# A four-part transformer kernel: order tables of the first attention and of the last feed-forward part, and a split maximum

## The chip, the cores and the metric

The kernel runs on one core of a Trainium2 chip. The metric is the device time of one execution in microseconds (us), as the median of several runs. A core has five engines that run their own instruction streams and meet at semaphores: TensorE (PE: matmuls and transposes; PEld is its weight load), VectorE (DVE), ScalarE (ACT), GpSimd (POOL) and SyncE (SP), which here only issues DMAs.

## The reference

Four sublayers, each added to the residual x of 4 batches x 512 tokens x 512 channels; all in float32:

```python
x = x + tanh(g_xattn[0]) * L0_xattn(layernorm(x), ctx, wq, wk, wv, wo, ...)   # 16 heads of 128, 4 key heads, RoPE, causal, 64 context keys
x = x + tanh(g_ffn[0])   * L0_ffn(layernorm(x), ...)                          # 16 experts, top 4, and a shared expert
x = x + tanh(g_xattn[1]) * L1_xattn(layernorm(x), ctx, mask, ...)             # 16 heads of 32 over 64 context keys, int8-like q and out
x = x + tanh(g_ffn[1])   * L1_ffn(layernorm(x), w1, g1, w2, g2, w3, g3)

def L1_ffn(x):                       # D = 512, H = 2048
    h = silu(linear_bit(x, w1, g1)) * linear_bit(x, w2, g2)
    return linear_bit(h, w3, g3)
def linear_bit(x, w, g):
    xq = act_quant(rmsnorm(x, g))    # scale 127 / max|row|, clipped from below; round
    wq = round(tanh(w / mean|w|)) * arctanh(mean|w|)      # values -1, 0, 1 times a constant
    return xq @ wq.T
```

## The kernel before, in words

The first attention (`attention0_stage`) runs in 64 slots, one for a group of 4 query heads with its key head and a tile of 128 tokens; the 16 tiles of the first key head come first. Every engine walks a table of steps that is written by hand: one string for each kind of slot, where the kind is the slot's number modulo 4 (`ACT_ORDER`, `DVE_ORDER`, `POOL_ORDER`, `PE_ORDER`; the first slot and what lies before and behind the 64 have strings of their own). The kind also says how many keys a tile sees: 192, 320, 448 or 576 for the kinds 0 to 3. All matmuls of float32 data are made of three products of high and low halves. The letters that matter here, for the softmax of slot s unless said otherwise:

- `S` (PE) scores of head i into PSUM; `M` (DVE, L689) their negated maximum; `e` (ACT, L577) exp with the row sum; `N` (DVE, L714) its reciprocal, and for head 3 also the product (L717); `p` (POOL, L803) the product with the reciprocal for heads 0 and 1; `n` (ACT, L582) the same for head 2.
- `P` (PE) transposes of the probabilities of slot s-1, piece i; `g` (ACT, L592 or L589) their copy out of PSUM; `V` (PE, L954, L951) the product with the values; `o` (ACT, L596) and `B` (DVE, L743) high and low half of the result; `W` (PE) the output projection.
- `k` and `q` (PE) the projections of slot s+2; `v` on ACT (L610 to L612) squares the key half and copies the values, `v` on DVE (L748, L750) is the rotation of k, after which piece 0 of `q` may use the PSUM bank that follows. `K` and `T` (PE, L958, L963) transpose k and q of slot s+1, `k` and `t` on ACT (L600, L604) and DVE (L727, L732) copy them; the next slot's scores wait for the last of these. `f` (ACT) and `E` (DVE), `x`, `q` and `r` belong to the norms and the rotation of q.
- `w` (ACT, L561) copies the next weight block to its high half, four pieces of 128 x 512, in a slot of kind 1 (output weights, slots 1, 17, 33, 49) or kind 2 (query weights, slots 14, 30, 46); POOL's `w` (L782) makes the low half of each piece.
- `j`: work for the last sublayer rides along. In 15 slots from 2 to 22 ACT sums pieces of its weights. In 24 slots from 25 to 60 DVE turns two pieces of 128 x 512 into -1, 0 and 1 (`j0`, `j1`, each L707 and L711). In kind order 0 to 3 these are 7, 5, 5 and 7 slots.

TensorE transposes go through two PSUM banks in turn (`TR`), so that a transpose waits for the copy of the one two before it; the projections, V and W go through two banks in turn as well (`A`).

The last sublayer (`attention1_ffn1_stage`, the functions called `feed`) runs on 16 tiles of 128 tokens, again with one string per engine: `PE_FEED`, `ACT_FEED`, `DVE_FEED`, `POOL_FEED`, and joins (`DVE_JOIN` and others) for the slots in which it starts up beside the second attention. `P` (L2528) are the up and gate products in 4 pieces, `s` (ACT) the silu, `g` (DVE, L2384) the product h, `h` (POOL, L2163) h times g3, `H` (DVE, L2388 and L2392) the largest absolute value of the row of 2048, `t` (POOL, L2173, L2174) two powers of the mean square, `M` (DVE, L2396 to L2398) the scale, `r` (ACT, L2274) the rounding in two halves, `U` (PE, L2541) the transposes of that, `R` (DVE, L2405) their copies to bfloat16, `Y` (PE, L2550) the down product of 16 matmuls, and `X` (DVE, L2410) its addition to x. `T`, `x`, `c`, `b`, `m`, `q`, `y`, `v`, `a`, `z` are the norm of the following tile and the mean square.

Of the kernel before, what the change touches and what calls it, by code (L numbers as in the profile page):

```python
# [24 lines left out]
F32 = mybir.dt.float32  # L25
# [23 lines left out]
E = 16  # L49
# [75 lines left out]
def attention0_stage(nc, x, ident, tri, gates, xT, xh, xl, next_weights, next_loaded, xn_dram, x_in, ctx_in, wq_in, wk_in, wv_in, wo_in, wkc_in, wvc_in, qw_in, kw_in, g_xattn, g_ffn,  # L125
# [17 lines left out]

    ACT_ORDER = {"last": "g0 g1 g2 g3 g4 o L", -3: "z0 z1 r0 r1 r2 r3 x u w c0",
# [7 lines left out]


    DVE_SLOT = "M0 M1 N0 L D X A j0 l v M2 N1 N2 M3 N3 k t B j1 E"
    DVE_ORDER = {"last": "A0 A1 X0 D X1 r0 A2 X2 r1 A3 X3 r2 r3 B", -3: "A0 A1 X0 A2 X1 A3 X2 X3 b u c0 w0 c1 w1", -2: "v A E", -1: "z v X k t E A l", "first": "M0 M1 N0 X A v M2 N1 N2 M3 N3 k t E",
                 0: DVE_SLOT, 1: DVE_SLOT, 2: DVE_SLOT, 3: DVE_SLOT}

# [112 lines left out]
    with ExitStack() as ctx:  # L270
        s_ = Scope(nc, ctx, "a0")
        raw = s_.sb("raw", [P, KD, 512])
        whi = s_.sb("whi", [P, 2, KD, 512], F32R)
# [51 lines left out]
        A = s_.ps("A", [P, 2, 512])  # L325
# [49 lines left out]
        with nc.Block() as block:  # L375
# [136 lines left out]
            def _(act):  # L512
# [3 lines left out]
                def do(name, i, s, m):  # L516
# [4 lines left out]
                    if name == "r" and s < SLOTS and row(s, 5, i) is not None:  # L521
                        t = row(s, 5, i)
# [3 lines left out]
                    if name == "u" and (s == BEGIN or s % PERIOD == PERIOD - 3):  # L526
                        t = 0 if s == BEGIN else s + 3
# [26 lines left out]
                    if name == "w" and (s == BEGIN or s % PERIOD in (1, PERIOD - 2)):  # L554
                        part = 1 if s % PERIOD == 1 else 0
                        t = 0 if s == BEGIN else s + (2, -1)[part]
                        if live(t, 0):
                            until(act, raw_loaded, loads(part), t, m)
                            until(act, (q_full, wo_full)[part], (tile, opened)[part], t - 1, m)
                            for k in range(KD):  # L560
                                act.activation(whi[:, part, k], raw[:, k], ACT.Copy).then_inc(whi_ready, 1)  # L561
                    if name == "j" and (s, i) in SUMS:
# [1392 lines left out]
def attention1_ffn1_homes(nc, kept, right, sb):  # L1955
# [25 lines left out]
    for name, shape, dt in (  # L1981
            ("f_xq", [P, 2, 2, D], F32), ("f_cx", [P, 2, D], F32), ("over_biases", [P, 1207], F32), ("junk", [P, F1 // 512, 512], BF16),
            ("over_wo", [P, KD, D], BF16), ("h", [P, 2, F1], F32), ("hqT", [P, 2, F1 // P, P], BF16), ("over_values", [P, 1608], F32),
            ("hg", [P, 2, F1 + 1], F32), ("over_p", [P, 2], F32), ("hq", [P, 2, F1], F32)):
        h[name] = sb(kept, f"f_{name}", shape, dt)
# [9 lines left out]
def attention1_ffn1_stage(nc, x, x_loaded, ident, gates, wT, sq, bq, gsw, gbo, mask, kbd, vbd, g12, g3, w12T, w3T, at, out, prefetch, homes):  # L1995
# [21 lines left out]

    PE_FEED = "P0 P1 U0 P2 U1 P3 T0 Y0"

# [3 lines left out]

    DVE_FEED = "M0 X0 b0 g0 m0 g1 R0 g2 R1 g3 H0 x0 H1"

# [18 lines left out]
    POOL_JOIN = {13: "B0.15 s0.13 fy0.0 A0.11 fy1.0 fp0.0",  # L2044
# [40 lines left out]
    with ExitStack() as ctx:  # L2085
# [28 lines left out]
        def part(c):  # L2114
            return slice(c * 512, (c + 1) * 512)
# [4 lines left out]
        with nc.Block() as block:  # L2120
# [158 lines left out]
            def _(ve):  # L2279
# [74 lines left out]
                def feed(name, n, s):  # L2354
# [60 lines left out]
            def _(pe):  # L2415
# [96 lines left out]
                def feed(name, n, s):  # L2512
# [187 lines left out]
```

## Time and profile before

| | |
|---|---|
| median of 3 runs | 1870.31 us (1869.50 to 1870.43) |
| time of the profiled execution | 1871.33 us |
| its span, first to last instruction | 1869.5 us |
| granted TensorE clock, mean | 0.984 |
| busy PE, DVE, ACT, POOL | 93%, 63%, 56%, 52% |
| first attention (slots) | 47 to about 1000 us |
| last sublayer alone | about 1657 to 1866 us |

The shares are means over the whole span. A matmul's end is modelled, so PE's busy time is no measure of how full it is: in the slots one reads from where to where a slot lasts and which wait stands in it. A row of the timeline gives start, duration, engine, line, operation, what it writes and reads, and in brackets how long the engine stood idle before it and who ended that.

### The profile page before, as it was taken

The numbers are of one execution on the slowest core, as the hardware profiler recorded it, in microseconds if no ns is written. First come the engines' busy times: TensorE is split into PE (matmuls) and PEld (weight loads), VectorE is DVE, ScalarE is ACT, GpSimd is POOL, SyncE is SP. The second block draws the span as 40 slices with busy tenths as digits, with TensorE's granted clock in tenths as the row PEclk, the third lists the DMA queues.
The fourth block names the chain that finished last, engine by engine and source line by source line (L and its number), as shares of the span: only waits on it lengthen the run. The fifth ranks groups of instructions, "written<-read, shape, count | busy, mean of one in ns | idle before, by whom it ended". The sixth has DMA issues, their size and how long they took to land. (4 is left out here: it accounts for less than half of the span.)

```text
span 1869.5 us, 28380 instructions
## 1 busy us (share of the span) xinstructions
PE 1741.5 (93%) x10015; PEld 1355.0 (72%) x10052; DVE 1181.8 (63%) x2415; ACT 1038.8 (56%) x2334; POOL 975.1 (52%) x864
## 2 busy tenths in 40 slices
PE   6999999999999999999998999989999778879997
PEld 4777887777877778777775888879999556634443
DVE  5666555557556776567766657634334678868885
ACT  3566666655655555545554422146665367767875
POOL 5644565445654456545541100048888356657774
PEclk9999999999999999999999999999999889999999
DMA  7111111111111111012122100167889660000000
GB/s 250 48 54 51 51 36 57 55 24 51 36 41 45 51 48 50 19 32 56 53 85 92 63 23 23 45 231 209 227 247 273 160 142 1 1 7 18 24 23 23
DMA packets 113611, 141.36 MB, mean 76 GB/s; under 512 B 38000, under 2 KB 68720, under 8 KB 113280
## 3 DMA queue, kind: packets, MB, share of 16 engines
q1 hardware_dynamic: 106304, 122.76, 21.0%
q0 software_dynamic: 7168, 16.78, 4.3%
q8 instruction: 82, 1.34, 0.3%
q14 instruction: 57, 0.47, 0.1%
HBM read 104.91 MB, written 29.36 MB: 72 GB/s over the span
## 5 line engine op out<-in xcount | busy, mean ns | idle before, releaser
L787 POOL TENSOR_TENSOR a_xcl<-xT,a_xch 128x512 fp32r<-128x512 f32 x64 | 87.3, 1365 | 323.4 <-ACT a_xch L571 323.4
L689 DVE TENSOR_REDUCE a_nmax<-a_S 128x1 f32<-128x192 f32 (+3 forms) x256 | 135.5, 549 | 83.0 <-PE a_S L897 82.8
L954 PE MATMUL a_A<-a_pT,a_vf 128*128 128x512 f32 x320 | 168.0, 607 | 6.5 <-ACT a_pT L592 6.5
L577 ACT ACTIVATE a_pr_odd<-a_S,a_nmax 128x320 f32<-128x320 f32 (+1 forms) x128 | 80.6, 631 | 149.9 <-DVE a_nmax L689 149.8
L120 PE MATMUL a_A<-a_wlo,a_xch 128*128 128x512 f32 x256 | 143.9, 562 | 14.0 <-DVE a_qb L750 11.4
L577 ACT ACTIVATE a_pr_even<-a_S,a_nmax 128x192 f32<-128x192 f32 (+1 forms) x128 | 67.0, 526 | 123.7 <-DVE a_nmax L689 123.4
L120 PE MATMUL a_S<-xl,xh 128*128 128x288 f32 (+3 forms) x320 | 121.8, 381 | 9.7 <-DVE xl L732 5.0
L1612 POOL TENSOR_TENSOR e_wlo<-expert_raw,e_whi 128x1408 fp32r<-128x1408 f32 x31 | 100.3, 3235 | 50.2 <-ACT e_whi L1784 48.0
L2528 PE MATMUL f_HH<-w12T,f_f_xqT 128*128 128x512 bf16 x496 | 117.5, 383 | 6.9 <-DVE f_h L2384 3.8
L714 DVE RECIPROCAL a_rec<-a_rs 128x1 f32<-128x1 f32 x256 | 41.2, 161 | 120.1 <-ACT a_pr_odd L577 67.1
L120 PE MATMUL e_GUP<-e_xgl,e_whi 128*128 128x256 f32 (+1 forms) x384 | 110.4, 287 | 4.3 <-DVE e_xgl L1840 2.7
L2163 POOL TENSOR_TENSOR f_hg<-f_h,g 128x512 f32<-128x512 f32 x64 | 81.4, 1272 | 52.1 <-DVE f_h L2384 52.1
L121 PE MATMUL e_GUP<-e_xgh,e_wlo 128*128 128x256 f32 (+1 forms) x384 | 108.6, 283 | 0.0
L122 PE MATMUL e_GUP<-e_xgh,e_whi 128*128 128x256 f32 (+1 forms) x384 | 108.3, 282 | 0.0
L120 PE MATMUL a_A<-a_wlo,a_oth 128*128 128x512 f32 x256 | 104.2, 407 | 2.8 <-DVE a_otl L743 2.8
L592 ACT ACTIVATE a_pT<-a_TR 128x512 f32<-128x512 f32 x160 | 94.8, 593 | 11.6 <-PE a_TR L938 10.8
L122 PE MATMUL a_A<-a_whi,a_xch 128*128 128x512 f32 x256 | 100.8, 394 | 0.0
L121 PE MATMUL a_A<-a_whi,a_xcl 128*128 128x512 f32 x256 | 100.7, 393 | 0.0
L122 PE MATMUL a_A<-a_whi,a_oth 128*128 128x512 f32 x256 | 100.6, 393 | 0.0
L121 PE MATMUL a_A<-a_whi,a_otl 128*128 128x512 f32 x256 | 100.4, 392 | 0.0
L796 POOL TENSOR_TENSOR a_qa<-a_qa,a_qb 128x640 f32<-128x640 f32 x64 | 100.3, 1567 | 0.0
L121 PE MATMUL a_S<-xh,xl 128*128 128x288 f32 (+3 forms) x320 | 98.8, 309 | 0.0
(417 smaller groups left out, 5593.9 us busy)
## 6 DMA issues: line engine op xcount, KB each, us to landing
a_pw<-in_L_ffn_w_dram SPq DMA_DIRECT2D x96, 256.0 KB, 2.8
expert_raw<-in_L_ffn_w_gate_dram SPq DMA_DIRECT2D x16, 704.0 KB, 8.1
expert_raw<-in_L_ffn_w_up_dram SPq DMA_DIRECT2D x16, 704.0 KB, 9.9
expert_raw<-in_L_ffn_w_down_dram SPq DMA_DIRECT2D x16, 512.0 KB, 10.3
tern<-a_tern SPq DMA_DIRECT2D x48, 128.0 KB, 1.8
x_res<-in_x_dram SPq DMA_DIRECT2D x4, 1024.0 KB, 9.2
a_raw<-in_L_xattn_wq_dram SPq DMA_DIRECT2D x4, 1024.0 KB, 6.1
a_raw<-in_L_xattn_wo_dram SPq DMA_DIRECT2D x4, 1024.0 KB, 5.5
```

The source lines that it names most:

```text
L120: pe.matmul(out, lhs_hi, rhs_lo, start=first, stop=False)
L121: pe.matmul(out, lhs_lo, rhs_hi, start=False, stop=False)
L122: return pe.matmul(out, lhs_hi, rhs_hi, start=False, stop=last)
L577: act.activation(pr[s % 2][:, i, 0:keys(s)], pair(s, i), ACT.Exp, bias=nmax[:, s % 2, i:i + 1], accum_out=rs[:, s % 2, i:i + 1]).then_inc( ...
L592: act.activation(pT[:, i % 2], bank, ACT.Copy).then_inc(pT_ready, 1)
L689: ve.tensor_reduce(nmax[:, s % 2, i:i + 1], pair(s, i), AX.X, ALU.max, negate=True).then_inc(s_max, 1)
L787: pool.tensor_tensor(xcl[:, t % 2], xT[:, :, tok(t)], xch[:, t % 2].bitcast(F32), ALU.subtract).then_inc(xlo_ready, 1)
L796: pool.tensor_tensor(qa[:, t % 2], qa[:, t % 2], qb[:, t % 2], ALU.add).then_inc(q_add, 1)
L954: pe.matmul(bank, vf[:, par(t), i], pT[:, i % 2], start=i == 0, stop=False)
L1612: pool.tensor_tensor(wlo[e % 2][q, cs], raw[q, e % 2, cs], whi[e % 2][q, cs].bitcast(F32), ALU.subtract).then_inc(gu_lo, 1)
L2163: pool.tensor_tensor(hg[:, u, part(n)], h[:, u, part(n)], g3[:, part(n)], ALU.mult).then_inc(hg_ready, 1)
L2528: last = pe.matmul(HH[pair_of(s, n)][j][:], f_xqT[:, u, j * KD + k], w12T[j][:, k, part(n)], start=k == 0, stop=k == KD - 1)
```

## The change

Three things are changed. In the first attention the tables of ACT and DVE for the four kinds of slot get another order. On ACT the copies `g` of transposes come before the exponential `e2`, and the four weight copies `w` become steps of their own, `w0` to `w3`, spread over the slot. On DVE the two operations of `j0` move behind the rotation of k (`v`) and behind `N1`, and so ahead of `M2`; in kind 1, `M3` also comes ahead of `N2`. In the last sublayer the down product is issued as 4 and 12 matmuls with the transposes `T` of the next norm between them; DVE copies the second half of the rounded row (`R1`) before `g2`, and takes the maximum of the row's first half before `g3`; and the maximum of the second half, one reduction of 1025 columns, becomes one of 512 and one of 514.

```diff
-                 1: "x e0 e1 j0 g0 j1 v u e2 r g1 n w j2 e3 k t o f",
+                 1: "x e0 e1 j0 g0 w0 j1 v u w1 r g1 w2 e2 e3 n w3 j2 k t o f",
...
-    DVE_SLOT = "M0 M1 N0 L D X A j0 l v M2 N1 N2 M3 N3 k t B j1 E"
+    DVE_SLOT = "M0 M1 N0 L D X A l v N1 j0 M2 N2 M3 N3 k t B j1 E"
...
@@ -555,10 +555,10 @@
                         if live(t, 0):
-                            until(act, raw_loaded, loads(part), t, m)
-                            until(act, (q_full, wo_full)[part], (tile, opened)[part], t - 1, m)
-                            for k in range(KD):
-                                act.activation(whi[:, part, k], raw[:, k], ACT.Copy).then_inc(whi_ready, 1)
+                            if i == 0:
+                                until(act, raw_loaded, loads(part), t, m)
+                                until(act, (q_full, wo_full)[part], (tile, opened)[part], t - 1, m)
+                            act.activation(whi[:, part, i], raw[:, i], ACT.Copy).then_inc(whi_ready, 1)
...
-    PE_FEED = "P0 P1 U0 P2 U1 P3 T0 Y0"
+    PE_FEED = "P0 P1 U0 P2 U1 P3 Y0 T0 Y1"
...
-    DVE_FEED = "M0 X0 b0 g0 m0 g1 R0 g2 R1 g3 H0 x0 H1"
+    DVE_FEED = "M0 X0 b0 g0 m0 g1 R0 R1 g2 H0 g3 x0 H1 H2"
...
+    Y_HEAD = 4
...
                     if name == "H" and n == 1:
+                        ve.wait_ge(hg_ready, NC * s + 3)
+                        c.link(ve.tensor_reduce(hg[:, u, F1 + 1:F1 + 2], hg[:, u, part(2)], AX.X, ALU.max, apply_absolute_value=True))
+                    if name == "H" and n == 2:
                         ve.wait_ge(hg_ready, NC * s + NC)
                         c.order()
-                        c.link(ve.tensor_reduce(amh[:, u:u + 1], hg[:, u, 1024:F1 + 1], AX.X, ALU.max, apply_absolute_value=True))
+                        c.link(ve.tensor_reduce(amh[:, u:u + 1], hg[:, u, 3 * 512:F1 + 2], AX.X, ALU.max, apply_absolute_value=True))
...
                     if name == "Y":
-                        pe.wait_ge(hq_copied, 2 * (s + 1))
-                        if s > 0:
+                        pe.wait_ge(hq_copied, 2 * s + n + 1)
+                        if n == 0 and s > 0:
                             pe.wait_ge(f_x_done, s)
-                        else:
+                        elif n == 0:
                             pe.wait_ge(y_ready, NT)
-                        for k in range(F1 // P):
+                        for k in (range(Y_HEAD), range(Y_HEAD, F1 // P))[n]:
                             last = pe.matmul(Y[:], hqT[:, u, k], w3T[:, k], start=k == 0, stop=k == F1 // P - 1)
-                        last.then_inc(f_y_full, 1)
+                        if n == 1:
+                            last.then_inc(f_y_full, 1)
```

The other kinds of `ACT_ORDER` change in the same way: in kind 3, for one, `v e2 r g1 n g2` becomes `v r g1 e2 n g2`, and in kind 2 `g2` now stands before `e3`.

On DVE, slot 59 (kind 3) has these rows before, from the maxima of heads 0 and 1 to the reciprocal of head 3:

```order
L689 TENSOR_REDUCE a_nmax<-a_S 128x1 x2
L714 RECIPROCAL a_rec<-a_rs 128x1
L739 SCALAR_TENSOR_TENSOR x_res<-a_A,gates,x_res 128x512
L707 TENSOR_SCALAR a_xn<-a_pw,a_nthr 128x512
L711 SCALAR_TENSOR_TENSOR a_tern<-a_pw,a_thr,a_xn 128x512
L722 TENSOR_TENSOR xl<-a_kT,xh 128x64
L748 TENSOR_TENSOR a_qa<-a_A,a_cos_k 128x128
L750 TENSOR_TENSOR a_qb<-a_A,a_sin_k 128x128
L689 TENSOR_REDUCE a_nmax<-a_S 128x1
L714 RECIPROCAL a_rec<-a_rs 128x1 x2
L689 TENSOR_REDUCE a_nmax<-a_S 128x1
L714 RECIPROCAL a_rec<-a_rs 128x1
```

The same place on DVE in the changed kernel:

```order
L689 TENSOR_REDUCE a_nmax<-a_S 128x1 x2
L714 RECIPROCAL a_rec<-a_rs 128x1
L739 SCALAR_TENSOR_TENSOR x_res<-a_A,gates,x_res 128x512
L722 TENSOR_TENSOR xl<-a_kT,xh 128x64
L748 TENSOR_TENSOR a_qa<-a_A,a_cos_k 128x128
L750 TENSOR_TENSOR a_qb<-a_A,a_sin_k 128x128
L714 RECIPROCAL a_rec<-a_rs 128x1
L707 TENSOR_SCALAR a_xn<-a_pw,a_nthr 128x512
L711 SCALAR_TENSOR_TENSOR a_tern<-a_pw,a_thr,a_xn 128x512
L689 TENSOR_REDUCE a_nmax<-a_S 128x1
L714 RECIPROCAL a_rec<-a_rs 128x1
L689 TENSOR_REDUCE a_nmax<-a_S 128x1
```

The two operations of j0 (L707, L711) have moved from ahead of the rotation (L748, L750) to behind it and behind one reciprocal, and still stand ahead of head 2's maximum.

On ACT, slot 49 (kind 1, with the copies of output weights, L561) had them in one block ahead of head 3's exponential:

```order
L592 ACTIVATE a_pT<-a_TR 128x512
L610 ACTIVATE a_sq<-a_A 128x128
L611 ACTIVATE a_vf<-a_A 64x128
L612 ACTIVATE a_vf<-a_A 64x128
L577 ACTIVATE a_pr_odd,a_rs<-a_S,a_nmax 128x320
L589 ACTIVATE a_qT<-a_TR 64x256
L582 ACTIVATE a_pr_odd<-a_pr_odd,a_rec 128x320
L561 ACTIVATE a_whi<-a_raw 128x512 x4
L577 ACTIVATE a_pr_odd,a_rs<-a_S,a_nmax 128x320
L600 ACTIVATE xh<-a_TR 128x128
```

The same place on ACT in the changed kernel:

```order
L592 ACTIVATE a_pT<-a_TR 128x512
L561 ACTIVATE a_whi<-a_raw 128x512
L610 ACTIVATE a_sq<-a_A 128x128
L611 ACTIVATE a_vf<-a_A 64x128
L612 ACTIVATE a_vf<-a_A 64x128
L561 ACTIVATE a_whi<-a_raw 128x512
L589 ACTIVATE a_qT<-a_TR 64x256
L561 ACTIVATE a_whi<-a_raw 128x512
L577 ACTIVATE a_pr_odd,a_rs<-a_S,a_nmax 128x320 x2
L582 ACTIVATE a_pr_odd<-a_pr_odd,a_rec 128x320
L561 ACTIVATE a_whi<-a_raw 128x512
L600 ACTIVATE xh<-a_TR 128x128
```

Three of the four copies stand now ahead of the exponentials of heads 2 and 3 and one behind them, and the copy of a transpose (L589) comes before both exponentials.

On DVE, one tile of the last sublayer, from the second product h (L2384 here) to the scale, before:

```order
L2384 SCALAR_TENSOR_TENSOR f_h<-f_HH,f_al,f_sg 128x512
L2405 TENSOR_SCALAR f_hqT<-f_TB 128x1024
L2384 SCALAR_TENSOR_TENSOR f_h<-f_HH,f_al,f_sg 128x512
L2405 TENSOR_SCALAR f_hqT<-f_TB 128x1024
L2384 SCALAR_TENSOR_TENSOR f_h<-f_HH,f_al,f_sg 128x512
L2388 TENSOR_REDUCE f_hg<-f_hg 128x1
L2375 TENSOR_SCALAR f_f_xqT<-f_TB 128x1024
L2392 TENSOR_REDUCE f_ST<-f_hg 128x1
L2396 TENSOR_SCALAR f_ST<-f_ST,f_rooth 128x1
```

The same in the changed kernel, where the lines have other numbers (L2384 is L2385, L2388 is L2389, L2392 became L2392 and L2396):

```order
L2385 SCALAR_TENSOR_TENSOR f_h<-f_HH,f_al,f_sg 128x512
L2409 TENSOR_SCALAR f_hqT<-f_TB 128x1024 x2
L2385 SCALAR_TENSOR_TENSOR f_h<-f_HH,f_al,f_sg 128x512
L2389 TENSOR_REDUCE f_hg<-f_hg 128x1
L2385 SCALAR_TENSOR_TENSOR f_h<-f_HH,f_al,f_sg 128x512
L2376 TENSOR_SCALAR f_f_xqT<-f_TB 128x1024
L2392 TENSOR_REDUCE f_hg<-f_hg 128x1
L2396 TENSOR_REDUCE f_ST<-f_hg 128x1
L2400 TENSOR_SCALAR f_ST<-f_ST,f_rooth 128x1
```

Behind the last product h stand now a copy (L2376), a reduction of 512 and one of 514 columns, where a reduction of 1024, the copy and one of 1025 stood.

## Rows read from the trace of the kernel before

**Rows 1.** Windows: four slots without and with pieces, slots 47, 59, 49

```profile
core 0: us, PE busy (x) PEld busy (x) DVE busy (x) ACT busy (x) POOL busy (x), PEclk, DMA share, GB/s
702.42:760.05 57.63, 57.45 (x326) 46.66 (x326) 32.35 (x75) 34.48 (x89) 35.65 (x33) 1.00 0.13 41
882.56:944.09 61.53, 58.59 (x327) 46.62 (x326) 44.98 (x91) 31.14 (x84) 30.39 (x28) 1.00 0.19 53
744.10:760.05 15.95, 15.77 (x92) 12.62 (x91) 8.72 (x19) 8.55 (x22) 7.66 (x7) 1.00 0.00 1
926.83:944.09 17.26, 16.02 (x93) 12.53 (x91) 12.11 (x23) 8.45 (x23) 7.85 (x7) 1.00 0.16 47
776.50:790.10 13.60, 12.27 (x72) 10.20 (x71) 8.79 (x22) 9.43 (x25) 11.53 (x11) 1.00 0.13 35
```

**Rows 2.** Waits of PE in slots 56 to 59: total, times, longest

```profile
PE a_A L120 <- DVE a_qb L750: 1.9, 4, 0.6
PE a_A L954 <- ACT a_pT L592: 0.6, 1, 0.6
```

**Rows 3.** Timeline of DVE in slot 59

```profile
931.72 1.56 DVE L707 TENSOR_SCALAR a_xn<-a_pw,a_nthr 128x512 bf16<-128x512 f32 x1
933.32 1.52 DVE L711 SCALAR_TENSOR_TENSOR a_tern<-a_pw,a_thr,a_xn 128x512 bf16<-128x512 f32 x1
...
935.29 0.74 DVE L689 TENSOR_REDUCE a_nmax<-a_S 128x1 f32<-128x576 f32 x1
```

**Rows 4.** Timeline of POOL in slot 59

```profile
931.75 1.26 POOL L799 TENSOR_TENSOR a_qa<-a_qa,a_srq 128x640 f32<-128x640 f32 x1
932.96 1.33 POOL L803 TENSOR_TENSOR a_pr_odd<-a_pr_odd,a_rec 128x576 f32<-128x576 f32 x1
936.18 1.15 POOL L803 TENSOR_TENSOR a_pr_odd<-a_pr_odd,a_rec 128x576 f32<-128x576 f32 x1 [1.89 <-DVE a_rec L714]
```

**Rows 5.** Timeline of ACT in slot 59

```profile
936.07 0.74 ACT L577 ACTIVATE a_pr_odd<-a_S,a_nmax 128x576 f32<-128x576 f32 x1 [2.55 <-DVE a_nmax L689]
...
937.28 0.77 ACT L582 ACTIVATE a_pr_odd<-a_pr_odd,a_rec 128x576 f32<-128x576 f32 x1
937.95 0.59 ACT L592 ACTIVATE a_pT<-a_TR 128x512 f32<-128x512 f32 x1
```

**Rows 6.** Timeline of PE in slot 59: V2

```profile
939.80 1.02 PE L954 MATMUL a_A<-a_pT,a_vf 128*128 128x512 f32 x2
```

**Rows 7.** All instances of DVE's L707 and of L711

```profile
L707 DVE TENSOR_SCALAR a_xn<-a_pw,a_nthr x48: 476/478/1561, 420.4 to 960.9; 128x512 bf16<-128x512 f32 x48
L711 DVE SCALAR_TENSOR_TENSOR a_tern<-a_pw,a_thr,a_xn x48: 750/1136/1648, 421.6 to 961.4; 128x512 bf16<-128x512 f32 x48
```

**Rows 8.** Timelines of ACT and PE in slot 49

```profile
785.12 2.18 ACT L561 ACTIVATE a_whi<-a_raw 128x512 fp32r<-128x512 f32 x4
...
789.39 0.47 PE L120 MATMUL a_S<-xl,xh 128*128 128x448 f32 x1 [1.33 <-DVE xl L732]
```

**Rows 9.** Groups of PE, whole span: transposes of k

```profile
L958 PE MATMUL a_TR<-ident_f,a_qa 128*128 128x128 f32 x64 | 17.7, 276 | 0.9 <-ACT xT L524 0.9
```

**Rows 10.** All instances of DVE's L2396, one a tile

```profile
L2396 DVE TENSOR_SCALAR f_ST<-f_ST,f_rooth x16: 226/226/227, 1663.0 to 1856.1; 128x1 f32<-128x1 f32 x16
```

**Rows 11.** Timeline of one tile of the last sublayer

```profile
1774.71 0.62 PE L2535 MATMUL f_TB<-f_ident_h,f_f_xq 128*128 128x128 f16 x8 [0.46 <-ACT f_f_xq L2251]
...
1776.93 1.27 POOL L2163 TENSOR_TENSOR f_hg<-f_h,g 128x512 f32<-128x512 f32 x1 [0.44 <-DVE f_h L2384]
...
1778.49 1.22 DVE L2392 TENSOR_REDUCE f_ST<-f_hg 128x1 f32<-128x1025 f32 x1
1778.68 0.55 POOL L2174 TENSOR_TENSOR f_unrooth<-f_ssum,f_mhalf 128x1 f32<-128x1 f32 x1
...
1780.29 1.24 ACT L2274 ACTIVATE f_hq<-f_hg,f_big,f_rech 128x1024 f32<-128x1024 f32 x1 [2.25 <-DVE f_rech L2397]
```

**Rows 12.** Timeline of PE at the end

```profile
1858.94 0.62 PE L2541 MATMUL f_TB<-f_ident_h,f_hq 128*128 128x128 f16 x8 [0.51 <-ACT f_hq L2274]
1860.75 4.82 PE L2550 MATMUL f_Y<-w3T,f_hqT 128*128 128x512 bf16 x15 [1.18 <-DVE f_hqT L2405]
```

More of the change, by code:

```diff
@@ L140, in attention0_stage @@
                 3: "S0 S1 W0 W1 W2 W3 P0 k0 k1 S2 R P1 V0 q0 P2 V1 S3 P3 K V2 q1 T V3 q2 q3"}
-    ACT_ORDER = {"last": "g0 g1 g2 g3 g4 o L", -3: "z0 z1 r0 r1 r2 r3 x u w c0",
+    ACT_ORDER = {"last": "g0 g1 g2 g3 g4 o L", -3: "z0 z1 r0 r1 r2 r3 x u w0 w1 w2 w3 c0",
                  -2: "c1 x v h0 f h1",
@@ L147, in attention0_stage @@
                  "first": "x e0 e1 v d1 r e2 n e3 k t f",
[4 rows of a table removed]
-    DVE_SLOT = "M0 M1 N0 L D X A j0 l v M2 N1 N2 M3 N3 k t B j1 E"
[4 rows of a table added]
+    DVE_SLOT = "M0 M1 N0 L D X A l v N1 j0 M2 N2 M3 N3 k t B j1 E"
     DVE_ORDER = {"last": "A0 A1 X0 D X1 r0 A2 X2 r1 A3 X3 r2 r3 B", -3: "A0 A1 X0 A2 X1 A3 X2 X3 b u c0 w0 c1 w1", -2: "v A E", -1: "z v X k t E A l", "first": "M0 M1 N0 X A v M2 N1 N2 M3 N3 k t E",
-                 0: DVE_SLOT, 1: DVE_SLOT, 2: DVE_SLOT, 3: DVE_SLOT}
+                 0: DVE_SLOT, 1: "M0 M1 N0 L D X A v N1 j0 M2 M3 N2 N3 k t B j1 E", 2: DVE_SLOT, 3: DVE_SLOT}
     POOL_ORDER = {"last": "r0 r1 r2 r3", -3: "r0 r1 r2 r3 x w c0", -2: "x c1 r", -1: "q x r", "first": "x q p0 p1 r",
@@ L1983, in attention1_ffn1_homes @@
             ("over_wo", [P, KD, D], BF16), ("h", [P, 2, F1], F32), ("hqT", [P, 2, F1 // P, P], BF16), ("over_values", [P, 1608], F32),
-            ("hg", [P, 2, F1 + 1], F32), ("over_p", [P, 2], F32), ("hq", [P, 2, F1], F32)):
+            ("hg", [P, 2, F1 + 2], F32), ("over_p", [P, 2], F32), ("hq", [P, 2, F1], F32)):
         h[name] = sb(kept, f"f_{name}", shape, dt)
```

8 rows, old and new, of tables (ACT_ORDER, DVE_JOIN) are left out of this document.

## The prediction

> **What bounds the kernel now.** I read the page first. PE is busy 93% of the span, in the first attention and in the last sublayer alike, so time can only be won where PE stands idle between two matmuls, and an edit on ACT, DVE or POOL is worth what it takes from such a gap. I then cut the first attention into slots [rows 1]. Four slots without pieces (47 down to 44) take 57.63 us with PE busy for 57.45; four slots with pieces (56 to 59) take 61.53. The two riding operations of each slot, which stand on DVE, thus cost PE 3.90 us in four slots, 0.98 in each. In kind 3 alone it is 17.26 against 15.95, or 1.31. The slots with pieces number 24, so 24 x 0.98 = 23.4 us is the most that any order of DVE can win there. Slot 49, with its four weight copies, takes 13.60 with PE busy 12.27: an idle stretch of 1.33 [rows 1].
>
> The waits of PE say where the gap is [rows 2]. Before piece 0 of `q` it waits for the rotation of k (L750), 1.9 us in the four slots, up to 0.6 in one; and once 0.6 for ACT's copy `g1` (L592) before V. The timeline shows why: `j0` stands ahead of the rotation and takes 1.56 and 1.52 us [rows 3], while the shortest instances of the two take 476 and 750 ns [rows 7]. In that time POOL works on the rotation of q and on `p0` [rows 4]. L707 ends at 931.72 + 1.56 = 933.28, 0.27 after POOL's L799 ended (933.01); L711 ends at 934.84, 0.55 after POOL's L803 (934.29). Each is as long as POOL's work beside it, plus a rest.
>
> In the last sublayer I took the period: 16 scales `M` between 1663.0 and 1856.1, 15 periods of 12.87 us [rows 10]. One tile shows what closes the ring [rows 11]: POOL's last product ends at 1776.93 + 1.27 = 1778.20, the maximum of 1025 columns runs from 1778.49 to 1779.71, then the scale, then ACT's rounding at 1780.29, for which ACT had waited 2.25 us. PE has gaps around it, one of 0.46 before `T`.
>
> **The change part by part, kind 3.** I lay out slot 59 again. Without `j0` ahead of it the rotation runs at once, and PE's wait of 0.6 [rows 2] goes. PE wanted its result 0.6 before it came, and it now needs L711's end (934.84) no more: I put the end of rotation and `N1` 0.8 ahead of that, at 934.04 (an estimate; `j0` begins there). POOL's `p0` ran 1.33 under `j0` and takes 1.15 without it (the second L803 [rows 4]), so it ends at 932.96 + 1.15 = 934.11. L707 then ends 0.27 behind that, 934.38; `p1` runs 934.38 to 935.53; L711 ends 0.55 behind it, 936.08. `M2` (0.74 [rows 3]), which ran from 935.29, starts near 936.08: it is now what is late. `e2` (0.74 [rows 5]) ends at 937.6, the reciprocal, `n` (0.77) and `g2` (0.59) behind it at 939.15, so the product V2 starts at 939.2; before it was 939.80 [rows 6]. The gain is 0.6 and not 1.2: the port that POOL and DVE seem to share is as busy at the new place, and half of what the rotation gives back is lost to `M2`. Bounds for this kind: 0 (M2 0.6 later still) and 1.31 (all of it).
>
> The Trainium skill has a rule on this ("SBUF — State Buffer", section "Who interferes with whom"): DVE operations of the kind of L707 and L711 take a port pair that GpSimd uses too, and whoever issues first keeps it for the whole instruction. The rows agree that one is held up by the other; by that rule alone an L707 that is issued before `p1` would not be held at all, which is the third rival below.
>
> Kind 0: the same chain, V2 behind `g2`; the same layout gives 0.4 (bounds 0 and 1). Kind 1: `g` of the late transposes is not in the way, and `M2`, `M3`, `e2`, `e3`, `n`, `k`, `t` become the chain that the next slot's scores wait for; with `M3` ahead of `N2` I get 0.45 (0 to 1). Kind 2: PE's transposes `T` wait for the copy `g2`, whose `n` hangs on `e2` and on the late `M2`; here I get 0.4 more than before, a loss (-1 to +0.6). Sum over the 24 slots: 7 x 0.6 + 7 x 0.4 + 5 x 0.45 - 5 x 0.4 = 7.2 us.
>
> Weight copies in kind 1 (slots 17, 33, 49): 2.18 us of copies stood in one block ahead of `e3`, and the next slot's first scores waited 1.33 for DVE's L732, the end of the chain e3, N3, t [rows 8]. Now three copies of 0.55 each stand where ACT had idled (2.55 us before `e2` in slot 59 [rows 5]) and one behind `n`; I take 1.2 for each, 3.6 us (bounds 2 and 4). In slot 1 other things are late: nothing. In kind 2 the copies open the slot in both orders: nothing.
>
> The copies `g1` and `r` ahead of `e2`: in quiet kind-3 slots PE is idle for 15.95 - 15.77 = 0.18 [rows 1]; in four of them that is 0.8. In early slots it shortens the transposes' wait, of which one line alone has 0.9 [rows 9]; with the same in kind 3 and the last two slots, which have no later work to hide it, I take 2.5 (0.9 to 3). What it costs is `e2` later by one copy (0.59), which in quiet slots lies in ACT's idle time.
>
> Last sublayer: the maximum of the first 1024 columns on DVE moves ahead of `g3`, so behind h3 (1778.20) only 514 columns are left. By length, half of 1.22 and a fixed part, 0.65: ended at 1778.9. The scale then waits for POOL's unrooth, which ends at 1778.68 + 0.55 = 1779.23 [rows 11], and comes at 1779.28 in place of 1779.82: 0.54 a tile. PE must be able to follow. Its `T` gap of 0.46 closes, because four matmuls of `Y` fill it, so a period of 12.87 - 0.54 = 12.33 just fits over PE's own work, which I put at 12.87 - 0.46 = 12.4 less some small gaps of 0.1. The first period is bound by POOL's other root; 14.5 x 0.54 = 7.8, I take 7.7 (bounds 3, if PE has only half of it free, and 9). The extra instruction and the extra semaphore on DVE lie in idle time of an engine at 63%.
>
> The end: PE waits 1.18 us for the second copy `R` before `Y`, and starts at 1860.75 [rows 12]. Four matmuls can start when the first half is copied, and `R1` no longer stands behind others; the last `Y` starts earlier, but its matmuls there run under a clock that has fallen after PE's idle stretch. I take 0.8 (0.3 to 1.18).
>
> Sum: 7.2 + 3.6 + 0.8 + 2.5 + 7.7 + 0.8 = 22.6 us. The profiled execution's own time was 1871.33, its span 1869.5. 1871.33 - 22.6 = 1848.7. The median of the runs is 1.0 lower than the profiled time (1870.31), so the forecast is **1847.7 us**.
>
> **The rivals.** *The late `M2` eats the gain of the pieces.* If L707 and L711 together take 0.3 longer behind the rotation than I gave them, each kind comes out 0.3 lower: 7 x 0.3 + 7 x 0.1 + 5 x 0.15 - 5 x 0.7 = 0 in place of 7.2. For it: POOL's `p1` is as long as anything in [rows 4], and L707's longest instance is 1561 ns. Against it: at the old place it was no shorter. 1847.7 + 7 = 1854.7; with half of the sublayer's gain gone too, 1858.
>
> *The port is free at the new place.* If `j0` takes its 476 + 750 ns = 1.23 us [rows 7] and not 2.0, `M2` starts 0.7 earlier in each of 24 slots: 24 x 0.7 = 17, but no more than up to the ceiling of 23.4, so 16 more than my 7.2: 1831.7. For it: L707 comes directly behind `N1` in DVE's own stream, while POOL's `p1` first has to hear of it. Against it: `p0` is still running.
>
> *One part does not work.* If PE's own work in a tile is 12.8 and not 12.3, the sublayer gives 1 and the sum is 15: 1855. If the attention is held by a chain that I haven't seen, 14.1 falls to 4: 1858.
>
> *Slower.* In each slot with pieces `M2` is the place: if `j0` behind the rotation makes `g2` of the same slot later than it is now by more than 1 us, V2 and the next slot's scores are. `g2` ended at 938.54 here [rows 5], and by hand it ends at 939.15, of which V2 has hidden all; it would need 1.6 us more. The price then is 24 x 1.0 = 24 us against a gain of 15.4 from the rest: 1879. I see no row that long.
>
> *It does nothing:* every gain moved to a later wait, 1870.
>
> **How the numbers follow.** Forecast (1842 to 1853): 0.58. Late `M2`: 0.17. Port free: 0.10, and between it and the forecast 1837 to 1842. One part fails: 0.08. No change: 0.04. Slower: 0.03. The range from 1837 to 1858 leaves out the free port, the slower case and no change, with a part of the others, just under 2 in 10. About 0.2% (3.7 us) is what a measurement of this kernel can tell from no change; so faster 0.93, the same 0.04, slower 0.03.
>
> **What would show each step.** Right: PE's wait for L750 is gone from the slots with pieces; L707 and L711 stand behind L750, sum near 2.0 us, and `M2` 0.8 later than now; V2 waits for ACT's copy; kind 3 takes 16.7; slots 17, 33 and 49 take 12.4; the period of `M` is 12.3 to 12.4 with POOL's unrooth as its releaser; `Y` stands as 4 and 12 with `T` between. Wrong: L707 and L711 of 1.2 us (free port), or V2 or T waiting over 1 us for `g2` (late `M2`), kind 2 longer by more than 0.5, or a period above 12.7 with PE without gaps.

## The result

The changed kernel takes 1840.22 us, the median of 4 runs (1836.94 to 1841.86), against 1870.37 for the kernel before: a ratio of 0.9837, 95% interval 0.9825 to 0.9849. It is faster by 30 us; 22.6 were forecast. The profiled execution took 1841.86 with a span of 1840.1, so the two traces differ by 29.5 us of span (1869.54 and 1840.07 before rounding), and these the profile can place.

The windows of the changed kernel, in the same five stretches as [rows 1] (four slots without pieces, four with, slots 47, 59 and 49):

```profile
688.02:745.07 57.05, 57.05 (x327) 46.66 (x325) 32.71 (x75) 35.31 (x89) 35.63 (x33) 1.00 0.12 41
864.16:924.16 60.00, 57.55 (x327) 46.56 (x325) 41.25 (x90) 31.38 (x84) 30.10 (x28) 1.00 0.20 54
729.56:745.07 15.51, 15.51 (x93) 12.60 (x91) 8.73 (x19) 8.76 (x23) 7.66 (x7) 1.00 0.00 1
907.52:924.16 16.64, 15.54 (x93) 12.63 (x91) 11.04 (x23) 8.56 (x23) 7.89 (x7) 1.00 0.18 47
761.22:773.55 12.33, 12.25 (x72) 10.19 (x70) 8.89 (x22) 8.99 (x25) 11.23 (x11) 1.00 0.13 39
```

The first column behind the stretch is its length. Four slots with pieces are 1.53 us shorter (61.53 to 60.00), four quiet ones 0.58 (57.63 to 57.05), slot 49 1.27. So of the 1.53 that the slots with pieces gained, 0.58 is what the quiet ones gained as well; what the pieces cost fell from 3.90 to 2.95 in four slots. Kind 3 went from 15.95 to 15.51 without pieces, and from 17.26 to 16.64 with them. PE's waits in slots 56 to 59, where [rows 2] stood before (total, times, longest):

```profile
PE a_TR L958 <- ACT a_pT L592: 1.6, 2, 1.1
PE a_TR L963 <- ACT a_qT L589: 0.5, 1, 0.5
PE a_S L120 <- DVE xl L732: 0.3, 1, 0.3
```

The wait for the rotation (L750) is gone. In its place the transposes of k and q (L958, L963) wait for ACT's copy `g2`. That copy is late because `M2` is. DVE in slot 59, where [rows 3] stood:

```profile
914.65 0.15 DVE L714 RECIPROCAL a_rec<-a_rs 128x1 f32<-128x1 f32 x1
914.72 0.47 DVE L707 TENSOR_SCALAR a_xn<-a_pw,a_nthr 128x512 bf16<-128x512 f32 x1
915.22 1.52 DVE L711 SCALAR_TENSOR_TENSOR a_tern<-a_pw,a_thr,a_xn 128x512 bf16<-128x512 f32 x1
916.66 0.74 DVE L689 TENSOR_REDUCE a_nmax<-a_S 128x1 f32<-128x576 f32 x1
```

and POOL, ACT and PE beside and behind it, as in [rows 4 to 6]:

```profile
913.72 2.47 POOL L803 TENSOR_TENSOR a_pr_odd<-a_pr_odd,a_rec 128x576 f32<-128x576 f32 x2
```

```profile
917.43 0.74 ACT L577 ACTIVATE a_pr_odd<-a_S,a_nmax 128x576 f32<-128x576 f32 x1 [2.17 <-DVE a_nmax L689]
...
918.50 0.78 ACT L582 ACTIVATE a_pr_odd<-a_pr_odd,a_rec 128x576 f32<-128x576 f32 x1 [0.23 <-DVE a_rec L714]
919.18 0.58 ACT L592 ACTIVATE a_pT<-a_TR 128x512 f32<-128x512 f32 x1
```

```profile
918.20 0.60 PE L936 MATMUL a_TR<-ident_f,a_pr_even 128*64 128x128 f32 x4
919.90 0.30 PE L958 MATMUL a_TR<-ident_f,a_qa 128*128 128x128 f32 x1 [1.10 <-ACT a_pT L592]
```

L707 now runs free (0.47); L711 is held to 1.52 and ends 0.55 after the second POOL product (913.72 + 2.47 = 916.19, against 916.74), the same rest as in [rows 3] and [rows 4]. `j0` takes 2.02 us from start to end, the prediction had 2.04 (934.04 to 936.08). `M2` starts 9.14 us into the slot, the prediction had 9.25. Everything behind follows: e2, n, g2, and K waits 1.10.

In the last sublayer the period of the scale is 12.41 us (it was 12.97 in the middle of the stage). All instances of the reciprocal behind it, one a tile:

```profile
L2401 DVE RECIPROCAL f_rech<-f_ST x16: 167/167/168, 1643.2 to 1828.3; 128x1 f32<-128x1 f32 x16
```

DVE in one tile, where [rows 11] stood:

```profile
1766.32 0.70 DVE L2396 TENSOR_REDUCE f_ST<-f_hg 128x1 f32<-128x514 f32 x1 [0.20 <-POOL f_hg L2164]
1767.34 0.23 DVE L2400 TENSOR_SCALAR f_ST<-f_ST,f_rooth 128x1 f32<-128x1 f32 x1 [0.33 <-POOL f_unrooth L2175]
```

The maximum ends at 1767.02, and the scale waits a further 0.33 for POOL's second power, as predicted. The table shows where the two traces differ, slot by slot from the first matmul of one slot's causal scores to that of the next:

| | predicted | measured |
|---|---|---|
| 24 slots with pieces; kinds 0, 1, 2, 3 | 7.2; 2.8, 2.2, -2.0, 4.2 | 8.2; 2.8, 1.6, 0.1, 3.8 |
| slots 17, 33, 49 | 3.6 | 3.7 |
| slots 2 to 11 | part of 3.3 | 4.5 |
| other slots from 12 on | part of 3.3 | 4.2 |
| start, slots 0 and 1 | 0 | 0.3 |
| from the attention to the last sublayer | 0 | -0.9 |
| last sublayer, first scale to last | 7.7 | 8.0 |
| behind the last scale | 0.8 | 1.5 |
| sum | 22.6 | 29.5 |

### The profile page after: what moved, and what is told of

Same layout as the page of the kernel before. It is cut to its first block and busy times, and to the rows that moved or that the text cites. A ratio compares the mean times of both kernels' runs of the same rounds, so it can differ in the third digit from the quotient of the medians.

```text
span 1840.1 us, 28396 instructions
## 1 busy us (share of the span) xinstructions
PE 1728.0 (94%) x10015; PEld 1358.3 (74%) x10052; DVE 1160.0 (63%) x2431; ACT 1047.6 (57%) x2334; POOL 971.2 (53%) x864
## 5 line engine op out<-in xcount | busy, mean ns | idle before, releaser
L714 DVE RECIPROCAL a_rec<-a_rs 128x1 f32<-128x1 f32 x256 | 41.2, 161 | 108.6 <-ACT a_pr_even L577 58.3
L592 ACT ACTIVATE a_pT<-a_TR 128x512 f32<-128x512 f32 x160 | 94.7, 593 | 23.8 <-PE a_TR L938 22.6
```

Source lines behind the costliest of these rows:

```text
L592: act.activation(pT[:, i % 2], bank, ACT.Copy).then_inc(pT_ready, 1)
```

## The experiments

Two theories on the attention stood against each other: that the move of `j0` on DVE gives the gain of the slots with pieces (the prediction), or that ACT's order gives nearly all. Two kernels tell them apart, a third takes the sublayer out, a fourth goes for what is left.

**ACT's order alone.** DVE's tables are those of before.

```diff
-    DVE_SLOT = "M0 M1 N0 L D X A l v N1 j0 M2 N2 M3 N3 k t B j1 E"
+    DVE_SLOT = "M0 M1 N0 L D X A j0 l v M2 N1 N2 M3 N3 k t B j1 E"
```

> The changed kernel with DVE's tables of before (the pieces ahead of the rotation of k), and ACT's new order. My theory, from the two traces: the order of ACT gives nearly all that the attention gained. In kind 3 a slot with a piece had two waits, 0.63 for the rotation and 0.61 for g1 behind e2; the first stays (quiet slot 15.51 + 0.63 = 16.14), the second goes, so kind 3 takes 16.1 to 16.2 and not 16.64. Kind 0 near 16.1, kind 2 near 14.65, kind 1 12.5 to 13.0. Then the move of j0 is worth between -4 and +2 us: 1836 to 1842. Rival, my prediction's term: the move of j0 is what gives the 8.4 us of the slots with pieces: 1848 to 1849.

Measured 1844.14 (1842.51 to 1845.47), ratio to before 0.9853 (0.9837 to 0.987). Slots 2 to 11 and the quiet ones of kinds 0 and 3 take the same as in the changed kernel. The windows of slots 56 to 59, slot 59, slot 58:

```profile
868.32:929.13 60.81, 58.23 (x326) 46.53 (x325) 45.11 (x90) 32.10 (x84) 30.40 (x28) 1.00 0.20 54
912.76:929.13 16.37, 15.76 (x92) 12.49 (x91) 12.11 (x23) 8.67 (x23) 7.85 (x7) 1.00 0.17 48
897.59:912.76 15.17, 14.21 (x79) 11.55 (x78) 12.10 (x24) 7.79 (x21) 7.84 (x7) 1.00 0.19 54
```

Kind 3 is 16.37 here, shorter by 0.27 than with the move; kinds 0 and 1 are longer by 0.25 and 0.3, kind 2 by 0.53, where PE waits longer for the rotation (0.96 in slot 58, 0.47 in the kernel before). PE's only waits of some length in slots 56 to 59:

```profile
PE a_A L120 <- DVE a_qb L750: 2.4, 4, 1.0
```

Of the 8.2 us of the slots with pieces, ACT's order alone gives 5.5, and the move adds 2.7. Another 2.7 come from the kind-1 slots without pieces, above all the three with weight copies (1.8), where DVE's new `M3` ahead of `N2` counts. So ACT's order gives most but not "nearly all" of the attention's gain: the time lies between the two theories' ranges, nearer to that of the first.

**DVE's order alone.**

```diff
-                 3: "x e0 l e1 j0 g0 j1 v r g1 e2 n g2 j2 e3 g3 k t o f"}
+                 3: "x e0 l e1 j0 g0 j1 v e2 r g1 n g2 j2 e3 g3 k t o f"}
```

The other kinds go back in the same way.

> The changed kernel with ACT's order of before (g1 and r behind e2; the four weight copies in one block ahead of e3 in kind 1), and DVE's new tables. Theory (ACT's order matters): the quiet kind-3 slots are back at 15.95, slots 2 to 11 give 4.5 us back, the three slots with weight copies 3.7, the other quiet ones 3.9; in the slots with pieces g1 stands behind an e2 that comes 0.66 later than before, so V1 waits 1.2 in kind 3 and nothing of their 8.4 us is left: 1840 + 20 = 1860 or more, up to 1866. Rival (DVE's order gives the gain of the pieces alone): 1852.

Measured 1889.54 (1888.09 to 1894.29), ratio to before 1.0107 (1.0088 to 1.0127): slower than the kernel before by 19 us, although the last sublayer's gain is in it. Both theories missed. The slots with pieces take 29.1 us more than in the changed kernel, 21 more than before. Slots 56 to 59 and slot 59:

```profile
903.42:968.07 64.65, 57.91 (x326) 46.71 (x325) 41.62 (x90) 30.97 (x84) 29.70 (x28) 1.00 0.19 51
950.12:968.07 17.95, 15.77 (x92) 12.63 (x91) 11.12 (x23) 8.45 (x23) 7.90 (x7) 1.00 0.16 45
```

PE's waits in slots 56 to 59, and PE's row of the longest:

```profile
PE a_A L954 <- ACT a_pT L592: 5.4, 3, 2.2
PE a_TR L963 <- ACT a_qT L589: 1.3, 1, 1.3
```

```profile
961.42 1.12 PE L954 MATMUL a_A<-a_pT,a_vf 128*128 128x512 f32 x2 [2.18 <-ACT a_pT L592]
```

ACT in slot 59:

```profile
960.05 0.74 ACT L577 ACTIVATE a_pr_odd<-a_S,a_nmax 128x576 f32<-128x576 f32 x1 [3.23 <-DVE a_nmax L689]
...
960.78 0.59 ACT L592 ACTIVATE a_pT<-a_TR 128x512 f32<-128x512 f32 x1
```

ACT idles 3.23 us on the late `M2`, with `g1` queued behind `e2`, and V1 waits 2.18. The size: V1 waited 0.6 before, the removed wait for L750 brings PE there 0.6 earlier, and `M2` is 0.7 later, 1.9 together. I had counted only the last of these as new. This is the slower rival's mechanism, a late `M2` that makes a copy and a product late (`g1` and V1 here, where the prediction looked at `g2`), in the kernel that lacks ACT's half of the change.

**The attention alone.** The last sublayer is that of before, its tables and its code; of the tables:

```diff
-    PE_FEED = "P0 P1 U0 P2 U1 P3 Y0 T0 Y1"
+    PE_FEED = "P0 P1 U0 P2 U1 P3 T0 Y0"
```

> Only the tables of the first attention are new, the last sublayer is that of before. Theory (the parts add, and the last sublayer has 8.0 us of shorter periods and 1.4 behind its last tile): 1840.2 + 9.4 = 1849.6. Rival (the 0.85 us that were lost between the attention and the last sublayer belong to one of the parts): 1848.8 or 1850.5.

Measured 1848.49 (1847.92 to 1851.0), ratio 0.9878 (0.9862 to 0.9895): 8.3 us above the changed kernel. The parts add within the scatter of the runs.

**`j0` split around `M2`.**

```diff
-    DVE_SLOT = "M0 M1 N0 L D X A l v N1 j0 M2 N2 M3 N3 k t B j1 E"
+    DVE_SLOT = "M0 M1 N0 L D X A l v N1 j0 M2 J0 N2 M3 N3 k t B j1 E"
```

`J0` is the second operation (here L714); kind 1 has it at the same place.

> The changed kernel, with the second operation of j0 (L711) moved behind M2 on DVE, the first (L707) left where it is. Theory (the late M2 makes e2, n and g2 late and that is all that is left of the cost of the pieces): M2 comes 1.4 us earlier, K's wait of 1.10 in kind 3, 0.50 in kind 0, T's 0.51 in kind 2 and the scores' 0.35 in kind 1 go, at most 7 x 1.1 + 8 x 0.5 + 5 x 0.5 + 5 x 0.35 = 16 us: 1824 to 1828. Rival (L711 behind M2 is held by POOL as long, and N2 behind it becomes as late): 1836 to 1842.

Measured 1818.65 (1818.13 to 1819.0), ratio 0.9721 (0.9704 to 0.9737): 21.6 us faster than the changed kernel. Slots 56 to 59 and slot 59:

```profile
845.70:902.74 57.04, 57.04 (x326) 46.65 (x325) 39.49 (x90) 31.77 (x84) 30.12 (x28) 1.00 0.21 58
887.23:902.74 15.51, 15.51 (x92) 12.59 (x91) 10.46 (x23) 8.66 (x22) 7.88 (x7) 1.00 0.18 52
```

```profile
894.43 0.47 DVE L707 TENSOR_SCALAR a_xn<-a_pw,a_nthr 128x512 bf16<-128x512 f32 x1
894.82 0.75 DVE L689 TENSOR_REDUCE a_nmax<-a_S 128x1 f32<-128x576 f32 x1
895.48 0.97 DVE L714 SCALAR_TENSOR_TENSOR a_tern<-a_pw,a_thr,a_xn 128x512 bf16<-128x512 f32 x1
896.47 0.16 DVE L717 RECIPROCAL a_rec<-a_rs 128x1 f32<-128x1 f32 x1
```

A slot with pieces now lasts as long as one without: 57.04 against 57.05. The pieces cost nothing once one held operation no longer stands ahead of `M2`, and behind it that operation takes 0.97 and not 1.52. In the slots this is 18.5 us against the changed kernel; 3.1 more are the start of the attention (last section). That `M2` was what the pieces still cost is shown.

**Both operations behind `M2`**, in all kinds.

```diff
-    DVE_SLOT = "M0 M1 N0 L D X A l v N1 j0 M2 N2 M3 N3 k t B j1 E"
+    DVE_SLOT = "M0 M1 N0 L D X A l v N1 M2 j0 N2 M3 N3 k t B j1 E"
```

> The changed kernel with both operations of j0 behind M2 on DVE and ahead of N2. Theory (only what stands ahead of M2 costs; N2 is wanted about 0.9 us behind M2, when e2 has ended): L707 0.5 and L711 0.8 to 1.5 put N2 0.4 to 1.0 later than in the split kernel, and n and g2 with it, so part of the waits comes back: 7 x 0.6 and some tenths elsewhere, 1820 to 1827. Rival (N2 has slack): 1818 to 1820. Rival (POOL holds both operations there): 1830 or more.

Measured 1827.67 (1825.32 to 1828.05), ratio 0.9768 (0.9751 to 0.9784). Kinds 0 and 3 are as short as with the split, kind 2 is 0.16 longer and kind 1 0.64 in most slots, 3.8 us over all slots with pieces. The traces place 3.2 more in the start and 0.5 in the slots with weight copies; 1.6 lie between the attention and the last sublayer, where the two programs are the same, so they are scatter (last section). L707 and L711 take 0.93 and 0.75 there. My price for kind 3 (0.6) was wrong, it has slack; kind 1, where `M3` is behind `j0` too, has none.

**The weight copies in a block.**

```diff
-                 1: "x e0 e1 j0 g0 w0 j1 v u w1 r g1 w2 e2 e3 n w3 j2 k t o f",
+                 1: "x e0 e1 j0 g0 j1 v u r g1 e2 n w0 w1 w2 w3 j2 e3 k t o f",
```

> The changed kernel with the four weight copies of kind 1 in one block ahead of e3, as before. Theory (the block is what makes the next slot's scores wait): slots 17, 33 and 49 go from 12.14, 12.59 and 12.33 back to 13.6, so 3.7 us more: 1843.9. Rival (the earlier n and g1 alone do it): 1840 to 1841.

Measured 1846.95 (1845.25 to 1850.59), ratio 0.9881 (0.9863 to 0.9899). Slot 49:

```profile
764.15:778.00 13.85, 12.25 (x72) 10.20 (x70) 8.78 (x22) 9.56 (x25) 11.53 (x11) 1.00 0.11 34
```

The three slots give 4.5 us back and not 3.7: they are 0.25 longer than before. Here `n` waits 0.43 for the reciprocal `N2`, which now stands behind `M3`, and the block behind `n` begins 0.25 later in the slot than before (8.87 us against 8.62). Of the 3.7, then, no part is left without the new places of the copies. They are needed, but not alone enough: with ACT's new order and DVE's old one (the first run) slots 33 and 49 take 13.10. This edit also puts `n` ahead of `e3`, so the block and that order are not told apart. The kind-1 slots with pieces give back 1.9; they have no copies, so there it is the rest of this table, above all `n` ahead of `e3`.

**The maximum in two pieces.**

```diff
-    DVE_FEED = "M0 X0 b0 g0 m0 g1 R0 R1 g2 H0 g3 x0 H1 H2"
+    DVE_FEED = "M0 X0 b0 g0 m0 g1 R0 R1 g2 H0 g3 x0 H1"
```

`H1` is one reduction of 1025 columns.

> The changed kernel with the maximum of h in two pieces as before: 1024 columns, then one of 1025 behind the last product of POOL; the down product stays in 4 and 12. Theory (the scale is the ring's late end, 0.54 each tile): M comes 0.54 later less the 0.3 that POOL's root holds it, no: the whole 0.54 is back, since 1.22 replaces 0.70 behind h3. Period 12.9 in place of 12.41, 14 periods: 1847. Rival (with the down product split, PE's own work sets the period): 1840 to 1842, period 12.4 to 12.55.

Measured 1845.67 (1842.07 to 1848.35), ratio 0.9862 (0.9842 to 0.9881). The period:

```profile
L2398 DVE RECIPROCAL f_rech<-f_ST x16: 167/167/168, 1645.8 to 1835.5; 128x1 f32<-128x1 f32 x16
```

In the middle of the stage it is 12.72: of the 0.56 a tile, 0.31 belongs to the third piece and the other 0.25 to the new order on DVE (`H0` ahead of `g3`, so the last reduction begins when POOL's product ends: within 0.04 in one tile here, 0.29 behind it in [rows 11]). The period lies between the two that were expected (12.9, and 12.4 to 12.55). The stage from first scale to last is 4.6 us longer than in the changed kernel.

**The down product in one block.**

```diff
-    PE_FEED = "P0 P1 U0 P2 U1 P3 Y0 T0 Y1"
+    PE_FEED = "P0 P1 U0 P2 U1 P3 T0 Y0 Y1"
```

What remains of the change is that the first four matmuls wait for the first copy `R` only.

> The changed kernel with PE's order P3 T0 Y0 Y1, so the sixteen matmuls of the down product stand in one block behind the transposes T, as before; the maximum stays in three pieces. Theory (PE has 0.41 of gaps in a period of 12.41, and T would wait some 0.6 for the rounding of the norm with nothing to fill it): period 12.6 to 13.0, 1843 to 1848. Rival (PE is not late, the wait is hidden): 1840.

Measured 1839.5 (1836.54 to 1845.26), ratio 0.9838 (0.9812 to 0.9864): no difference. The period is 12.41, though `T` waits as before:

```profile
1761.06 0.62 PE L2539 MATMUL f_TB<-f_ident_h,f_f_xq 128*128 128x128 f16 x8 [0.46 <-ACT f_f_xq L2252]
1761.52 3.62 PE L2554 MATMUL f_Y<-w3T,f_hqT 128*128 128x512 bf16 x16
```

**The scale waits for the first power only**, on top of the split `j0`.

```diff
-                        ve.wait_ge(rooth_ready, 2 * (s + 1))
+                        ve.wait_ge(rooth_ready, 2 * s + 1)
```

The wait for the second power stands ahead of the one operation that reads it.

> j0 split around M2 as before in this study, and in the last sublayer the scale waits for the first power of the mean square alone (the other one, which only the next factor reads, is waited for there). Theory (behind h3 the ring's end is POOL's second power, 0.3 us later than the maximum): M is 0.3 earlier and the period 12.1 to 12.2: 1818.65 less 3 to 4, so 1814.5 to 1816. Rival (PE, whose gaps are only 0.41 of 12.41, is reached first, or the gaps before U stay for another reason): 1817 to 1819.

Measured 1816.3 (1815.7 to 1818.47), ratio 0.971 (0.9692 to 0.9727), the fastest kernel of the study. The period is 12.19:

```profile
L2404 DVE RECIPROCAL f_rech<-f_ST x16: 167/167/168, 1622.4 to 1804.9; 128x1 f32<-128x1 f32 x16
```

That is 0.22 less a tile, but the first two periods are longer: from first scale to last the stage takes 182.5 us against 184.9 with the split alone, 2.4 less, and the medians differ by 2.3.

**And the down product in one block there**, by the same edit of `PE_FEED`.

> The kernel with j0 split and the scale waiting for the first power alone (1816.3), with the down product in one block behind T again. Theory (the split of the down product gives nothing as long as the scale's ring is longer than PE's work, but here PE is the bound): T's wait of 0.46 is no longer hidden, the period goes from 12.19 back to about 12.4, 14 periods, 1819 to 1820. Rival (it never matters): period 12.19, 1816.3.

Measured 1817.03 (1814.02 to 1819.48), ratio 0.9709 (0.9688 to 0.9729), the period still 12.20. The rival holds: placing `T` between 4 and 12 matmuls does nothing in either kernel.

## Why the prediction was right, and where its sizes were off

The direction and the mechanism of each large term hold; the time (1840.2) lies between the forecast and the lower end of the range. But it lies outside the forecast's own bracket (1842 to 1853), in the one that the prediction gave to a partly free port (1837 to 1842), and the port was not free: `j0` took its 2.02 us. The time came there through ACT's order, which was priced too low.

**Kind 3 by hand: right in its numbers, by luck in who earns them.** `M2` came to 0.1 us, and the gain is 0.62 for 0.6. One link was misread: the copy `g2` is waited for by the transpose of k, which goes through the same two banks, and not by V2. And the layout gave the 0.6 to the move of `j0`, while 0.44 of it is what kind 3 without pieces gained too, and with ACT's order alone kind 3 gained 0.89: there the move takes 0.27 back. The layout had no term for V1's wait of 0.6 for `g1` [rows 2], which ACT's order removes.

**The port.** L707 ran free (0.47) ahead of the second POOL product, and that product took 1.31 and not 1.15 (the row of 2.47 holds both, 1.14 and 1.31 with a step of 0.02 between); L711, issued 0.34 behind that product's start, was held to 0.55 behind its end. In the kernel before and in the changed one, all 24 L711 of `j0` end 0.55 behind a POOL product, and every L707 that is held ends 0.28 behind one. Each rest is 0.20 short of the operation's own time (0.75 and 0.48), so all of an operation but its first 0.2 us stands behind the other's end (an estimate from these four numbers). The rule of the Trainium skill ("SBUF — State Buffer", "Who interferes with whom": whoever issues first keeps the port) agrees with that. But the recorded start does not tell who was first when the two are close: in [rows 3] and [rows 4], L707 starts 0.03 ahead of L799 and is held all the same. So the port was free for L707 at the new place and not for L711.

**Kind 2: wrong sign.** I gave it -0.4 and it has +0.04. Its `T` waits 0.5 for the copy, as said, but the wait removed (0.47 for the rotation in slot 58) is as large; I had counted only a part of it.

**Kind 1: right in size** (0.43 for 0.45), but its `g` was in the way. In slot 57 before, PE waited 0.44 for that copy (L589) and only 0.17 for the rotation; [rows 2] leaves this row out:

```profile
PE a_TR L963 <- ACT a_qT L589: 0.4, 1, 0.4
```

**The weight copies: right in size**, 3.7 for 3.6. The prediction gave all of it to the new places of the copies on ACT; ACT's order alone gives 1.9, and 1.8 need DVE's order as well.

**The step that was too small:** "in quiet kind-3 slots PE is idle for 15.95 - 15.77 = 0.18". The slots gained 0.44 each. PE in slot 47, at V1, before and in the changed kernel:

```profile
753.33 1.12 PE L954 MATMUL a_A<-a_pT,a_vf 128*128 128x512 f32 x2 [0.18 <-ACT a_pT L592]
```

```profile
738.51 1.02 PE L954 MATMUL a_A<-a_pT,a_vf 128*128 128x512 f32 x2
```

V1 begins 9.29 us into the slot before and 8.95 now, 0.34 earlier, of which only 0.18 was recorded as idle: the modelled end of the transposes ahead of it covers the rest. And its two matmuls take 1.12 behind the wait and 1.02 without, another 0.10. Together that is the 0.44, so the idle time of a row understates what a wait costs. In slots 2 to 11 the same order gave 4.5 us, where the prediction had 2.5 for these and the last two slots together, built on one recorded wait of 0.9. The kernel with DVE's order alone gives these back (5.0 us in slots 2 to 11), so they belong to ACT's copies ahead of `e2`. Slots 2 to 11 and the other quiet ones gave 8.7 us for 3.3: this is 5.4 of the 6.9 us that the sum missed.

**Who earns it.** The prediction gave the 7.2 us to the move of `j0`. The runs share it otherwise: ACT's order alone brings the kernel to 1844.1, DVE's alone to 1889.5, both to 1840.2. Each engine's order is worth something else depending on the other's. With ACT's old order the move costs 21 us in the slots with pieces; with the new one it gives 2.7. That their sum came out (8.2 for 7.2) is therefore luck in part: the larger share was earned by a step that the prediction priced for the other slots only. The slower rival (3 in 100) was a real mechanism, and ACT's order is what keeps it away; I worked its price from the finished pair only.

**The last sublayer: right in size** (8.0 for 7.7) and in its releaser, POOL's second power. The condition "PE must be able to follow" was too tight: I put PE's own work at 12.3, and the period reaches 12.2 with `T` waiting. So the fill of its gap, which the prediction counted as needed, is needed in no kernel here.

**The end:** 1.5 for 0.8. PE's row of the last down product, as in [rows 12]:

```profile
1832.19 3.91 PE L2554 MATMUL f_Y<-w3T,f_hqT 128*128 128x512 bf16 x15 [0.22 <-issue]
```

The wait of 1.18 is 0.22 now, and the matmuls take 3.91 in place of 4.82. The first was in the term; the second is the clock, and the prediction put no size on it. Before, the granted clock was 0.53 over the first 3.6 us of these matmuls; now it was 0.87 over them, and 0.50 over the transposes ahead, which took 2.17. In the kernel with the maximum in two pieces it was 1.00 over both, behind a wait of 2.83, and all that lies behind the last scale took 1.0 us less than in the changed kernel. So where the clock falls moves this term by about 1 us; whether the new order or the single execution decided it is not shown.

**Small slips in the sums:** 4 x 0.18 is 0.7 and not 0.8, and with a sublayer that gives 1 the sum is 15.9 and not 15. Neither moves the forecast by more than 0.1 us.

## What to carry to other kernels

A filler operation on a side engine should stand where the next thing behind it is not on PE's path, and a filler of two operations can be placed as two: splitting it around one reduction gave 18.5 us in the slots, on top of the 2.7 from moving it whole. Orders of two engines that wait for each other are one edit: price each half without the other, since half of a good change can cost more than the whole gives: in the slots with pieces DVE's half alone cost 21 us, and both together gave 8.2. Take the worth of a removed wait from the lengths of the stretches with and without it, not from the idle time recorded in it.

## What the hardware showed that was not expected

The changed kernel's runs scatter over 5 us. Part of it is in slots 0 and 1, behind PE's idle stretches of about 4 and 1.2 us. Two profiled kernels whose program is the same there, the one with both operations of `j0` behind `M2` and then the one with `j0` split (columns as in [rows 1]; the granted clock is the third number from the end):

```profile
48.00:52.00 4.00, 4.00 (x14) 2.72 (x13) 1.64 (x6) 0.82 (x3) 3.34 (x3) 0.66 0.00 2
...
64.00:68.00 4.00, 3.87 (x13) 2.69 (x14) 1.87 (x8) 2.86 (x8) 4.00 (x5) 0.57 0.00 0
```

```profile
48.00:52.00 4.00, 4.00 (x15) 2.15 (x14) 1.18 (x5) 0.82 (x3) 2.88 (x3) 0.99 0.00 0
...
64.00:68.00 4.00, 4.00 (x22) 3.27 (x21) 2.66 (x8) 3.62 (x11) 4.00 (x5) 1.00 0.00 0
```

With nearly the same idle stretches ahead (4.2 and 1.2 us, 4.1 and 1.2), the granted clock was 0.66 and then 0.57 in the one (partly at 1.2 GHz), 0.99 and 1.00 in the other (2.4 GHz), and slot 2 began at 72.6 and 69.4 us. That is 3.2 us that no order table made, more than several of the terms above: the two programs differ only in slots from 25 on. The two ran on different chips, but the chip doesn't explain it: on that of the second, profiled kernels with the same program up to there began slot 2 at 69.4, 69.4, 71.8, 72.4 and 72.8 us. The stretch from the last slot of the attention to the first scale scatters too: 678.2 to 680.0 us in four kernels with the same program there. Terms of 1 to 3 us can thus be read from the lengths of single slots, which repeat within a few hundredths, but hardly from the time of a whole run. Why the clock falls in one and not in the other stays open.
